# An expert's weights in two transfers of 4 KB per partition instead of one of 8 KB

## The reference, cut to what matters

```python
# x: T tokens of width D=512; 64 experts; I=256; CAP=128 tokens per expert at most; K=6 experts per token
h  = relu(einsum('ecd,eid->eci', xd, w1)) ** 2      # w1: "up" weights, 256 x 512 per expert
yd = einsum('eci,edi->ecd', h, w2)                  # w2: "down" weights, 512 x 256 per expert
out[tok] += yd[expert, slot] * gate                 # rows of one expert are distinct tokens
# and for all tokens a shared expert: relu(x @ su.T)**2 @ sd.T, hidden width 1024
```

## Time and profile before

| | us |
|---|---|
| three runs | 992.01, 998.65, 1001.14 |
| median | 998.65 |
| profiled execution, own time | 993.44 |
| its span | 991.6 |
| first scatter issued (from the span's start) | 577.7 |
| last scatter issued | 985.2 |

### The profile page before, as it was taken

The page is one execution under the profiler, slowest core; times in us unless marked ns, Lnnn a source line. Parts: engine busy times, 40 slices in busy tenths (PEclk is TensorE's granted clock), DMA queues, the critical chain, the costliest instruction groups (busy, mean ns, idle before and its releaser), DMA issues. The chain is left out here.

```text
span 991.6 us, 14608 instructions
## 1 busy us (share of the span) xinstructions
PE 899.6 (91%) x4947; PEld 627.3 (63%) x4947; DVE 551.5 (56%) x1143; ACT 232.7 (23%) x716; POOL 463.8 (47%) x512
## 2 busy tenths in 40 slices
PE   4899999998899999989999999999999699979980
PEld 3566666664677777766444486867677567656750
DVE  4787888867688888887889323322232223222220
ACT  1465656461400000122110021211121111111100
POOL 1644352533588888630282334444543454444432
PEclk9989999999999999999999999999999899989995
DMA  7300000020533333033007557987998799979763
GB/s 291 112 1 2 1 2 1 2 75 1 200 111 96 97 99 95 1 137 118 0 1 260 184 144 246 280 267 218 292 263 258 214 264 267 266 218 266 234 149 53
DMA packets 44126, 143.41 MB, mean 145 GB/s; under 512 B 7280, under 2 KB 11632, under 8 KB 35120
## 3 DMA queue, kind: packets, MB, share of 16 engines
q1 hardware_dynamic: 26352, 96.46, 26.4%
q0 software_dynamic: 14912, 37.76, 19.5%
q10 hardware_dynamic: 2816, 8.59, 2.3%
HBM read 114.36 MB, written 28.43 MB: 144 GB/s over the span
## 5 line engine op out<-in xcount | busy, mean ns | idle before, releaser
L1359 PE MATMUL ps<-arena 128*128 128x128 f32 (+4 forms) x2128 | 518.2, 402 | 11.0 <-DVE arena L813 5.7
L1359 PEld LDWEIGHTS ps<-arena 128*128 128x128 f32 x2128 | 340.6, 192 | 151.6 <-issue 105.3
L596 POOL DMA_INDIRECT out<-arena,scatter_rows x64 | 101.2, 1581 | 220.0 <-DMA out<-arena,scatter_rows 147.9
L1294 DVE TENSOR_TENSOR arena<-arena 128x256 f32<-128x256 f32 x64 | 27.4, 428 | 223.0 <-ACT arena L798 201.8
L1359 PE MATMUL ps<-features_T,arena 128*128 (+2 forms) x640 | 116.0, 338 | 0.0
L646 ACT ACTIVATE arena<-ps 128x512 f32<-128x512 f32 (+1 forms) x137 | 78.5, 590 | 130.2 <-DVE residual L1258 56.8
L1359 PEld LDWEIGHTS ps<-features_T,arena 128*128 128x128 f32 x640 | 84.7, 188 | 37.3 <-issue 37.3
L468 POOL TENSOR_TENSOR arena<-arena 128x512 f32<-128x512 f32 x48 | 49.3, 1059 | 89.2 <-DVE arena L833 89.2
L585 POOL DMA_INDIRECT arena<-token_rows,gather_rows x64 | 66.4, 1037 | 38.1 <-DVE gather_rows L1287 27.1
L798 ACT ACTIVATE arena<-ps 128x256 f32<-128x256 f32 x64 | 24.6, 384 | 253.8 <-PE ps L1359 237.8
L656 ACT ACTIVATE arena<-arena 128x128 f32<-128x128 f32 x192 | 74.0, 389 | 16.7 <-DVE arena L821 16.7
(11 more groups left out here) (176 smaller groups left out, 1080.0 us busy)
## 6 DMA issues: line engine op xcount, KB each, us to landing
arena<-wexp SPq DMA_DIRECT2D x48, 1024.0 KB, 6.4
residual<-wexp SPq DMA_DIRECT2D x16, 1024.0 KB
arena<-toeplitz_rows SPq DMA_DIRECT2D x32, 256.0 KB, 3.1
arena<-ctxE SPq DMA_DIRECT2D x32, 192.0 KB, 3.2
residual<-x SPq DMA_DIRECT2D x4, 1024.0 KB, 5.5
token_rows<-arena SPq DMA_DIRECT2D x16, 256.0 KB, 2.3
arena<-suT ACTq DMA_DIRECT2D x1, 2048.0 KB, 7.7
arena<-sdT ACTq DMA_DIRECT2D x1, 2048.0 KB, 12.4
```

The lines of the kernel that those rows point to most:

```text
L596: pool.indirect_dma_start(out, bass.IndirectOffsetOnAxis(ap=idxs[:, s % NY:s % NY + 1], axis=0), ysb[:, s % NY, :], None, compute_op=ALU.a ...
L1359: ins = TE.matmul(out_ap, lhsT, rhs, start=(n == 0), stop=(n == len(pairs) - 1))
```

## The change

```diff
-        wexp_loaded = [sem(f"expert_weights_slot{k}_loaded") for k in range(NW)]
+        w_halves = [[sem(f"expert_{half}_weights_slot{k}_loaded") for half in ("up", "down")] for k in range(NW)]
...
             def load_expert(s, i):
-                sp.dma_start(wring[s], a["wexp"][ds((i * UE + s) * P, P), :]).then_inc(wexp_loaded[s], 16)
+                for k in range(2):
+                    part = slice(k * DC * I, (k + 1) * DC * I)
+                    sp.dma_start(wring[s][:, part], a["wexp"][ds((i * UE + s) * P, P), part]).then_inc(w_halves[s][k], 16)
...
             def hidden(s, i):
                 pe.wait_ge(empt[FE.bank(("xgT", s))], FE.drained(("xgT", s), i))
-                pe.wait_ge(wexp_loaded[s], i * 16 + 16)
+                pe.wait_ge(w_halves[s][0], i * 16 + 16)
...
                 pe.wait_ge(y_ready[(s - 2) % NY], i * (UE // NY) + ((s - 2) // NY + 2))
+                pe.wait_ge(w_halves[s][1], i * 16 + 16)
                 product(ps[:, 4 + s % 2, :], ...
```

## The result

The changed kernel takes 1002.6 us, median of 20 runs (995.5 to 1010.1), and the kernel before 993.45 in 20 runs (983.9 to 1002.1): a ratio of 1.010 with a 95% interval of 1.0076 to 1.0123. It is slower by 1%. I had forecast a small gain, of 4.8 us. The profiled execution took 1003.18 us (span 1001.4), 9.7 more than that of before.

What follows compares the result with a forecast made beforehand. The prediction took POOL's chain of scatters to bound the kernel, with PE next. Its terms, -5.4 - 3.5 + 4.1 = -4.8 us, took 998.65 to 993.9, forecast as 994 us, with a range of 977 to 1010.

Steps and rivals of the forecast that it cites:

- What bounds the kernel: Expert stage: POOL's chain of scatters sets the end, PE next; weight traffic costs the chain 31.3 us.
- Part (3): DMA engines: twice as many weight rows cost 0.07 us per expert, 4.1 us in all; ends 0 and 12.2.
- Parts (1) and (2): Smaller weight rows beside the scatter gain 5.4 us (ends 0, 17.3), beside the gather 3.5 us (ends 0, 14.0).
- the sum: Whole kernel: -5.4 - 3.5 + 4.1 = -4.8 us.
- The turns: DMA engines beside the scatter: if turns between queues decide, halved rows halve the excess, giving 987.1 us; chance 0.28.
- Part (4): SP's queue: twice as many transfers and semaphores stay hidden and cost 0.
- Part (5): PE's waits: earlier up product gains nothing, new wait for down weights costs nothing; 0.
- nothing changes but the packets: Rival: no gain beside scatter or gather, only the rows' cost of 4.1 us, giving 1002.8 us; chance 0.19.
- The stalled ring: Rival: a semaphore amid the weights' queue waits beside scatter writes, adding 15.7 us, giving 1014 us; chance 0.12.

Runs made afterwards that it cites:

- e8: The kernel before without the 56 weight loads of the loop, all experts using the weights of the first eight: ratio 0.966 to before.
- g2: The changed kernel itself, run again on one chip beside others: ratio 1.008 to before.
- g3: The kernel before itself, run again on one chip beside others: ratio 1.000 to before.
- e4: The change, with the up and the down weights of an expert each in one piece of 512 KB in DRAM: ratio 1.003 to before.
- f1: The change, with each half padded by 256 B, so rows of a half lie 8704 B apart: ratio 1.000 to before.
- g1: The change, with 512 B of padding behind the down weights of each row, so rows of a half lie 8704 B apart: ratio 0.997 to before.
- h1: The change carried to four transfers with rows of 2 KB per expert, rows 8704 B apart: ratio 1.006 to before.
- e7: The kernel before plus a useless transfer of 128 rows of 512 B per expert: ratio 1.008 to before, 8.2 us slower for 14.5 us more engine time.
- f6: The kernel before with its load written as neighbouring 4 KB rows, which were joined, giving the packets of before: ratio 1.005 to before.
- e2: The kernel before, one transfer with rows of 8 KB, but 8704 B apart in DRAM: ratio 1.000 to before.
- e9: The kernel before with one transfer of 4 KB rows per expert, up and down weights each in one piece of 512 KB: ratio 1.001 to before.
- f7: The change, with the up product waiting for both halves and the down product for none: ratio 1.008 to before.
- g4: The change, with rows of a half 16384 B apart in DRAM: ratio 1.008 to before.
- e6: The kernel before with two experts' weights in one transfer of 2 MB, rows of 16 KB, after every second scatter: ratio 1.052 to before.

## Why the prediction was wrong

*What bounds the kernel*: right. The chain of scatters holds the whole difference, e8 shows that the weights cause its excess, and PE and SP wait as forecast. One reading was loose: I took the single engine that still moves at 767 for the one that the scatter waits for. By the packet records the last row of that scatter ended at 766.35, when the share was 0.31, some five engines; what moves after it is weights and gathered rows. POOL is released 1.4 us behind that row, and 1.1 us behind it in a cycle without weights (960.94 to 962.05).

*Part (3), the cost of the rows*, is the step that failed. "One cut is a third, 2.9% of 2.46, 0.07 us per expert": the engines' work grew by 0.24 (15.6 us over 64), above even the upper end of 0.21, and in the second trace of the change by 0.30 (g2 against g3). The row used for it, x at 396 GB/s, was of shorter rows read from another layout. The runs split it. Rows of 4 KB that lie well cost 0.10 to 0.13 per expert (e4 6.5 us, f1 8.4, g1 8.6 over 64), and the distance of 8192 B the rest, 0.11 to 0.16 (by the change against g1, and g2 against g1). So the size alone was priced too low as well: h1, with three cuts as in the row of x, pays 19.9 us over g3, 0.31 per expert, where I had 0.21. The description of the change says that each transfer now reads one half of each row of 8 KB; I listed the parts without asking what that does to the addresses in DRAM. The price was taken from the size of a row when its place changed too.

The Trainium skill has something near to this, which I didn't carry over: "DMA: Bandwidth & Descriptors", section "Latency and other measured facts", gives a loss of rate for row pitches of large powers of two, from 512 KiB up, in copies of rows of 16 KiB, and padding of the pitch as the cure. It has no figure for a pitch of 8 KiB. The runs here show a loss at 8 and 16 KiB, 180 to 185 ns for a row of 4 KB in the mean against 170 to 174, and the cure working with 512 B.

*Parts (1) and (2), the gain from smaller rows beside the scatter*, 8.9 us, are not shown at this size; that there is some gain has signs. Three runs have everything in them that I had put in the sum, and not the distance: g1 measures -3.0 us, f1 0, e4 +3.1, where the sum said -4.8. The mean is 0, and -4.8 lies outside the intervals of f1 and e4. They have 6.5 to 8.6 us more engine work, which at e7's price of 0.56 should cost 3.7 to 4.8 us. So, as an estimate, some 4 us came back from shorter rows, about half of what I forecast, or up to 8 at the price of 1.0 of the pairs above. The traces show a part of it. The longest expert cycle is 8.69 to 9.68 us with rows of 8 KB (before, g3, f6, e2, e7), 7.87 to 8.00 with rows of 4 KB that lie well (g1, f1, e4, e9), and 8.74 to 8.88 at 8192 and 16384 B (after, g2, f7, g4). The number of cycles over 7 us didn't fall as I had expected: six to eight of 58 with rows of 8 KB, six or seven with those of 4 KB that lie well, six to ten at the slow distances. And the gain doesn't grow with shorter rows: h1 is at +5.5 us with 20 us of added work, of which the price of 0.56 explains 11.

The turns themselves can be seen, which the prediction had left open between a row and some 9 to 17 descriptors. In the longest cycle of before, the last engine at work moves from 766.66 to 767.62, by the packet records, a row of weights (309 ns), a packet of gathered rows (178 ns), a row of weights, a packet of gathered rows. There the engine turns from queue to queue at every row or packet, not after the 8 rows of a transfer.

*Part (4)*: right. Two transfers and semaphores cost nothing that shows (e4 and f1 have them). The Trainium skill's rule of at least 1 MiB per DMA didn't bind here, where the queue has the next transfer waiting: e4 is at 1.003 and f1 at 1.000 with 512 KB each. Nor was a second fixed part of 2.0 us paid; the section that has it is about transfers that GpSimd issues, and these are SP's. *Part (5)*: right (f7).

*The sum*: -4.8 us were forecast. By the runs it is -3.0 to +3.1 for what I had listed (g1, f1, e4) and +8.3 to +10.6 for the distance that I hadn't (f7 against f1, g2 against g1); the 20 runs of the change give 9.2. No part and no rival names the cost of the distance, so it is luck that 1002.6 still lies in the range of 977 to 1010. The case "nothing changes but the packets" had the sign, with 4.1 us less than half of the size; that its 1002.8 meets the measured 1002.6 is luck too, since it was counted from 998.65, 5.2 above the median of 20 runs. The stalled ring, the rival on the slower side, was wrong: e4 and f1 have its semaphore in the middle and none of its cost.

## What to carry to other kernels

When a transfer is split, ask what each part now reads: two halves of a row by two transfers have gaps at the row's pitch, and at 8192 B that cost 7 to 12 us of engine time in 270, and about 1% of the kernel, where 512 B of padding on the host avoided it. If the DMA engines have little slack beside a serial chain (0.3 us in 5.5 here), each microsecond of added engine time cost 0.5 to 1 us here. The share of a queue times the span is a useful second judge of such a change beside the kernel's time, whose repeats differ by half a per cent: it was 260.5 to 265.5 us in four traces with the packets of before (before, e2, g3, f6) and 277.4 to 280.6 in three with the change's loads (after, f7, g2). A rate in one window of six us is a poor judge: 376, 385 and 419 GB/s in the same three.

## What the runs showed of the hardware that I had not expected

- A row of 4 KB takes 159 ns in the median wherever it lies, but in the mean over 64 loads 180 to 185 ns at a pitch of 8192 B, 184 at 16384, 174 at 8704, and 170 to 173 without gaps. The time of a row by size, in the median: 84 ns for 2 KB (h1), 159 for 4 KB, 309 for 8 KB, 611 for 16 KB (e6).
- A load into 64 partitions instead of 128 moves 213 GB/s instead of 426, at a DMA share of 1.01 in both, and the queue's engine time was 383 us instead of 262; the kernel took 1.078.
- Loads of 2 MB after every second scatter made the chain alternate between 8.2 and 5.7 us per cycle and cost 5%, at fewer packets and the same bytes.
- One transfer with two rows of 4 KB per partition, 256 B or 2048 B apart, took 1.021 in both builds, at 405 and 416 GB/s in the window of the back-to-back loads.
- When one late engine served two queues, it changed between them at every row or packet (the kernel before, 766.66 to 767.62).
